# Attention: the row maxima of two heads taken by one instruction over two neighbouring PSUM banks

## The chip, the cores and the metric

The kernel is one program on one core of a Trainium2 chip. Its five engines (TensorE, the matmul engine, PE in the profile; VectorE, DVE; ScalarE, ACT; GpSimd, POOL; SyncE, SP) each run their own list of instructions in order, and wait for each other through semaphores. The metric is the device time of one execution in microseconds (us); of the kernel before there are three runs, and one further execution with the profiler on, which all rows below come from.

## The reference, cut to what matters

The whole is two gated blocks on 32 sequences of 100 tokens of width 256: cross-attention, a mixture of experts routed by a recurrence (GRU), an alignment step, and a second mixture of experts. The change is in the first, the cross-attention, whose core is:

```python
q = (query @ Wq.T + bq).reshape(B, -1, HEADS, HEAD_DIM)     # 32 x 100 x 16 heads x 16
k = (key @ Wk.T + bk).reshape(B, -1, HEADS, HEAD_DIM)       # 32 x 361 x 16 x 16
v = (value @ Wv.T + bv).reshape(B, -1, HEADS, HEAD_DIM)
scores = jnp.einsum('bqhd,bkhd->bhqk', q, k) * scale
attn = jax.nn.softmax(scores, axis=-1)
out = jnp.einsum('bhqk,bkhd->bqhd', attn, v).reshape(B, -1, DIM)
return out @ Wo.T + bo
```

The softmax takes away each row's maximum over the 361 keys before the exponential: a maximum for each of 100 queries, 16 heads and 32 batches. The kernel's scores carry a negative scale, so that the maximum is taken as a minimum, and the exponential runs with scale -1.

## The kernel before, in words

Function `attention` (from L242) works batch by batch, 32 in all, and within a batch head by head, 16 slots h = 0 to 15. The order of each engine's instructions is written out by hand: on each engine a function `turn_of(b, u, first, last)` runs through the 16 slots, and a table of constants (L265 to L270) says in which slot what happens. The work is a software pipeline: while the heads of batch b are turned and multiplied, the projections of batch b+1 and the last steps of batch b-1 lie in between.

The life of one head:

- `scores` (L565): TensorE makes the scores of a group of four heads at a time. Each takes a strip of 32 rows of the array, so the four run side by side; each writes its own PSUM bank, `score[0]` to `score[3]`, 100 x 361 in float32. This happens in slots h = 2, 6, 10, 14, for the group that begins two slots later (in slot 6 heads 8 to 11; in slot 14 heads 0 to 3 of the next batch). It waits until the exponentials of the whole group before are done (`p_ready`), because these read the same four banks.
- `maximum` (L453): VectorE reduces one bank, 100 x 361, to 100 x 1 in `neg_max`. It waits for the score of its head (`s_psum`) and for the use of its place in `neg_max` eight heads earlier.
- `exponential` (L377): ScalarE writes the exponentials of the bank to `probs`, once the head's maximum is there (`max_ready`).
- `turn_probs` (L576): TensorE transposes `probs` in three parts of 121 keys (slot h for head h), when the exponential is done.
- The turned head is copied to `probsT`, an even head by VectorE (L505) and an odd one by ScalarE (`odd_out`, L387).
- `outputs` (L584): four heads times the values, 24 small matmuls, once a group.

Beside these a batch has: `project_keys`, `project_queries`, `project_values` for the next batch; `turn_back`, `divide` (reciprocal and product on VectorE, L462 and L464), `turn_attn`, `project_output` and the statistics for the batch before.

On VectorE a slot begins with the copy of an even head; then come the maxima that `MAXIMA[h % 4]` names, counted from the first head of the current group (4 and above is the next group); then the slot's other work. `MAXIMA = ((3,), (), (4,), (5, 6))` means: the first head of a group gets its maximum in slot 2 of the group before, the second and third in slot 3, and the fourth only in the next slot 0, after the copy of the even head there. ScalarE has the same kind of table: in slot 3 (after the copy of the odd head) the exponential of the next group's first head, in slot 0 the second and third, in slot 1 the fourth.

Of the kernel before, what the change touches and what calls it, by code (L numbers as in the profile page):

```python
# [7 lines left out]
F32 = mybir.dt.float32  # L8
# [3 lines left out]
ALU = mybir.AluOpType  # L12
ACT = mybir.ActivationFunctionType
AX = mybir.AxisListType

P = 128
B, S, DIM = 32, 100, 256
KV, KC = 361, 121
# [3 lines left out]
HEADS, HD = 16, 16  # L22
# [201 lines left out]
def at_least(engine, semaphore, value):  # L224

    if not isinstance(value, int) or value > 0:
        engine.wait_ge(semaphore, value)
# [14 lines left out]
def attention(nc, rows, mean, rstd, ctxT, weights, weights_in, x_rows, ident,  # L242
# [10 lines left out]
    with ExitStack() as ctx:  # L253
        def sb(name, shape, dt=F32):
            return ctx.enter_context(nc.sbuf_tensor("att_" + name, shape, dt))

        def ps(name):
            return ctx.enter_context(nc.psum_tensor("att_" + name, [P, 512], F32))

        def sem(name):  # L260
            return ctx.enter_context(nc.semaphore("att_" + name))

        BANKS, KEPT = 4, 8
# [2 lines left out]
        KEYS, VALUES = (1, 9), (11, 13, 15)  # L266
        FIRST_OUTPUTS, OUTPUTS = 4, {8: 1, 12: 2}
        SCORES = 2
        MAXIMA = ((3,), (), (4,), (5, 6))
        EXPONENTIALS = ((1, 2), (3,), (), (4,))  # L270
        wq, wk, wv, wo, bq_bk, mask_sb, bv_all, bo_gated, gate = weights
        c_in = [sb(f"c_in{u}", [P, KT, KVP]) for u in range(2)]
# [7 lines left out]
        neg_max = sb("neg_max", [S, KEPT])  # L280
# [4 lines left out]
        attn = sb("attn", [S, HEADS, HD])  # L285
        attnT = sb("attnT", [P, KT, S])

        score = [ps(f"score{n}") for n in range(BANKS)]
        turned = [ps(f"turned{n}") for n in range(2)]
        outs = ps("outs")  # L290
        misc = ps("misc")
# [9 lines left out]
        s_psum, max_ready, p_ready = sem("s_psum"), sem("max_ready"), sem("p_ready")  # L301
# [13 lines left out]
        def head_at(b, u, h, last):  # L315

            if h < HEADS:
                return b, u, h
            return None if last else (b + 1, 1 - u, h - HEADS)
# [116 lines left out]
        def _(dve):  # L436
            def normalized(b):
                at_least(dve, xnT_psum, b)
                normalize(nc, xn[:], rows_of(b), mean, rstd, b).then_inc(xn_ready, 1)

            def queries_out(b):
                dve.wait_ge(q_psum, b + 1)
                at_least(dve, q_ready, b)
                nc.vector.tensor_tensor(q_all[:], misc[:, 0:KT * S].rearrange("p (g s) -> p g s", g=KT),  # L444
                                        bq_bk[:, 0, :].unsqueeze(2).to_broadcast([P, KT, S]), ALU.add).then_inc(q_copied, 1)

            def values_out(b, u, m):
                dve.wait_ge(v_psum, 3 * b + m + 1)
                at_least(dve, o_psum, HG * b - HG)
                nc.vector.tensor_tensor(v[u][:, m, :, 0:HD], misc[0:KC, 0:DIM].rearrange("p (h d) -> p h d", h=HEADS),  # L450
                                        bv_all[0:KC, :].rearrange("p (h d) -> p h d", h=HEADS), ALU.add).then_inc(v_ready, 1)

            def maximum(b, u, h):  # L453
                dve.wait_ge(s_psum, HEADS * b + h + 1)
                at_least(dve, p_ready, HEADS * b + h + 1 - KEPT)
                nc.vector.tensor_reduce(neg_max[:, h % KEPT:h % KEPT + 1], score[h % BANKS][0:S, 0:KV], AX.X, ALU.min).then_inc(max_ready, 1)  # L456

            def divide(b):

                dve.wait_ge(back_psum, b + 1)  # L460
                heads = misc[0:S, :].rearrange("p (h j) -> p h j", h=HEADS)
                nc.vector.reciprocal(inverse[:], heads[:, :, HD]).then_inc(inverse_ready, 1)  # L462
                dve.wait_ge(inverse_ready, b + 1)
                nc.vector.tensor_tensor(attn[:], heads[:, :, 0:HD], inverse[:].unsqueeze(2).to_broadcast([S, HEADS, HD]),  # L464
                                        ALU.mult).then_inc(attn_ready, 1)

            def add_output(b, u):
                dve.wait_ge(bias_added, b + 1)
                dve.wait_ge(y_psum, b + 1)
                nc.vector.scalar_tensor_tensor(x1[u][:], misc[0:S, DIM:2 * DIM], gate[0:S, 0:1], rows_of(b),  # L470
                                               ALU.mult, ALU.add).then_inc(x1_ready, 1)

            def keep_output(b, u):
                dve.wait_ge(x1_ready, b + 1)
                at_least(dve, aggregated, b)
                nc.vector.tensor_scalar(rows_of(b), x1[u][:], 1.0, None, ALU.mult).then_inc(x1_kept, 1)
                nc.vector.bn_stats(stats[:], x1[u][:]).then_inc(stats_done, 1)

            def statistics_taken(b):
                dve.wait_ge(stats_done, b + 1)  # L480
                at_least(dve, stats_kept, b)

            def aggregate(b):
                nc.vector.bn_aggr(mean_var_now[:], stats[:]).then_inc(aggregated, 1)

            def keep_statistics(b):
                dve.wait_ge(aggregated, b + 1)
                nc.vector.tensor_scalar(mean_var[:, bass.ds(b, 1), :].rearrange("p a n -> p (a n)"), mean_var_now[:], 1.0, None, ALU.mult).then_inc(stats_kept, 1)
# [5 lines left out]
            queries_out(0)  # L494
            for m in range(3):
                values_out(0, 0, m)
            for h in range(3):
                maximum(0, 0, h)

            def turn_of(b, u, first, last):  # L500
                for h in range(HEADS):
                    if h % 2 == 0:
                        dve.wait_ge(t_psum, HEADS * b + h + 1)
                        at_least(dve, o_psum, HG * b + h // 4 - 1)
                        nc.vector.tensor_copy(probsT[h // 4 % 2][:, h % 4, :], turned[0][0:KC, 0:3 * S]).then_inc(even_ready, 1)  # L505
                    if h == TURN - 4 and not last:
                        normalized(b + 1)
                    for r in MAXIMA[h % 4]:
                        head = head_at(b, u, h - h % 4 + r, last)
                        if head:  # L510
                            maximum(*head)
                    if h == BACK and not first:
                        divide(b - 1)
                    if h == OUTPUT + 2 and not first:
                        statistics_taken(b - 1)
                    if h in VALUES and not last:
                        values_out(b + 1, 1 - u, VALUES.index(h))
                    if h == OUTPUT and not first:
                        add_output(b - 1, 1 - u)
                    if h == QUERIES and not last:  # L520
                        queries_out(b + 1)
                    if h == OUTPUT + 1 and not first:
                        keep_output(b - 1, 1 - u)
                    if h == OUTPUT + 2 and not first:
                        aggregate(b - 1)
                    if h == OUTPUT + 3 and not first:
                        keep_statistics(b - 1)

            pipelined(dve, B, turn_of)
            divide(B - 1)  # L530
            add_output(B - 1, 1)
# [2104 lines left out]
```

## Time and profile before

| | |
|---|---|
| time, median of 3 runs | 3348.98 us (3347.38 to 3350.77) |
| time of the profiled execution | 3356.15 us |
| its span, first to last instruction | 3354.5 us |
| mean granted TensorE clock | 0.945 |
| TensorE matmul busy, whole span | 2969.9 us (89%) |
| VectorE busy | 1424.3 us (42%) |
| ScalarE busy | 958.9 us (29%) |
| row maxima (L456) | 512 instructions, 250.1 us |

The attention stage lies in the first 750 us of the span. A start in the rows is in microseconds from the span's start; the number after it is the duration, of all merged instructions together where there are several (the x at the end is their count). Square brackets give how long the engine had been idle before and who released it. Busy TensorE time includes the overlap of one matmul with the next, so a short delay on TensorE can show as no idle time at all.

### The profile page before, as it was taken

The page shows a single profiled execution, that of the slowest core. Times are in us where ns is not written, and L with a number is a line of the kernel's source. Part 1 is how long each engine was busy: PE and PEld are TensorE (multiplying, and loading weights), DVE is VectorE, ACT ScalarE, POOL GpSimd, SP SyncE. Part 2 cuts the span into 40 slices and gives each one's busy share as a digit, 9 for nine tenths or more (in the row PEclk, how much of TensorE's full clock was granted, in tenths as well). Part 3 has the DMA queues.
Part 4 walks back from the last instruction along what each step waited for, and adds up shares of the span by engine and source line. Part 5 has one row for each costly group of instructions (what it writes and reads, how often), then busy time and mean ns, then how long its engine had stood idle before and what let it go on. Part 6 is the DMA issues. An engine that isn't in the chain of part 4 may idle for free. (4 is left out here: it accounts for less than half of the span.)

```text
span 3354.5 us, 72380 instructions
## 1 busy us (share of the span) xinstructions
PE 2969.9 (89%) x27712; PEld 1662.2 (50%) x27713; DVE 1424.3 (42%) x3167; ACT 958.9 (29%) x2643; POOL 815.3 (24%) x771
## 2 busy tenths in 40 slices
PE   5999999988999999999999999999999976008698
PEld 3666666653444444444444444458666644007454
DVE  4666666652222233333323333345222246985311
ACT  2555555543111111111111111122122236472111
POOL 1111001100222222232222222233444422004243
PEclk9999999987999999999999999999999988558699
DMA  6000000003000000000000000041222253005143
GB/s 225 24 21 20 21 23 23 23 11 128 23 16 23 17 23 17 23 17 17 22 17 23 17 23 17 23 176 53 43 45 45 45 148 119 0 0 198 46 115 72
DMA packets 81216, 163.02 MB, mean 49 GB/s; under 512 B 12056, under 2 KB 54936, under 8 KB 76408
## 3 DMA queue, kind: packets, MB, share of 16 engines
q1 hardware_dynamic: 55848, 102.34, 9.7%
q0 software_dynamic: 21504, 40.67, 5.5%
q10 hardware_dynamic: 3664, 17.04, 1.4%
q8 instruction: 162, 2.65, 0.3%
q14 instruction: 38, 0.31, 0.0%
HBM read 119.63 MB, written 40.37 MB: 48 GB/s over the span
## 5 line engine op out<-in xcount | busy, mean ns | idle before, releaser
L926 PE MATMUL gru_ps_rz<-whh,scratch 128*32 128x512 f32 x6400 | 707.4, 594 | 0.0
L734 POOL TENSOR_TENSOR scratch<-scratch 128x1024 f32<-128x1024 f32 (+3 forms) x246 | 369.6, 1527 | 818.5 <-DVE stat L748 657.6
L926 PEld LDWEIGHTS gru_ps_rz<-whh,scratch 128*32 128x32 f32 x6400 | 197.7, 110 | 452.1 <-issue 452.1
L931 PE MATMUL gru_ps_n<-whh,scratch 128*32 128x256 f32 x6400 | 363.6, 379 | 0.0
L855 DVE TENSOR_TENSOR scratch<-scratch,state 128x256 f32<-128x256 f32 x100 | 50.8, 508 | 661.1 <-ACT scratch L884 661.1
L931 PEld LDWEIGHTS gru_ps_n<-whh,scratch 128*32 128x32 f32 x6400 | 207.9, 110 | 180.1 <-issue 59.8
L380 ACT ACTIVATE att_probs<-att_score,att_neg_max 100x361 f32<-100x361 f32 x512 | 260.6, 568 | 122.2 <-DVE att_neg_max L456 122.1
L581 PEld LDWEIGHTS att_turned<-ident,att_probs 100*121 100x121 f32 x1536 | 210.3, 185 | 140.3 <-issue 105.9
L581 PE MATMUL att_turned<-ident,att_probs 100*121 100x100 f32 x1536 | 267.3, 287 | 11.8 <-ACT att_probs L380 5.0
L456 DVE TENSOR_REDUCE att_neg_max<-att_score 100x1 f32<-100x361 f32 x512 | 250.1, 525 | 56.0 <-PE att_score L573 56.0
L884 ACT ACTIVATE scratch<-gru_ps_rz 128x512 f32<-128x512 f32 x100 | 59.7, 597 | 720.3 <-PE gru_ps_rz L926 720.3
L903 PE MATMUL gru_ps_rz<-wih,scratch 128*32 128x512 f32 x1600 | 191.5, 596 | 2.2 <-POOL scratch L823 2.2
L2219 PE MATMUL e_ps_g<-align_reach,ident 32*121 32x101 f32 x64 | 10.9, 326 | 196.8 <-DVE align_reach L2031 195.3
L748 DVE TENSOR_REDUCE stat<-scratch 128x2048 f32 (+3 forms) x96 | 181.1, 1886 | 0.0
L505 DVE COPY att_probsT<-att_turned 121x300 f32<-121x300 f32 x256 | 119.0, 465 | 134.3 <-PE att_turned L581 134.1
L887 ACT ACTIVATE scratch<-scratch 128x256 f32<-128x256 f32 x100 | 41.7, 417 | 349.0 <-DVE scratch L859 349.0
L390 ACT COPY att_probsT<-att_turned 121x300 f32<-121x300 f32 x256 | 103.5, 404 | 131.9 <-PE att_turned L581 131.9
L857 DVE TENSOR_TENSOR scratch<-scratch,gru_ps_n 128x256 f32<-128x256 f32 x100 | 42.1, 421 | 231.7 <-PE gru_ps_n L931 231.7
L573 PE MATMUL att_score<-att_kT,att_qT 32*100 32x361 f32 x1024 | 112.3, 508 | 16.1 <-ACT att_probs L380 15.4
L356 POOL TENSOR_TENSOR att_qT<-att_q_all,att_head_mask 128x400 f32<-128x400 f32 x32 | 27.3, 853 | 379.8 <-DVE att_q_all L444 379.7
L1470 DVE COPY mix_room<-mix_ps_m 128x512 f32<-128x512 f32 x57 | 39.4, 691 | 187.7 <-PE mix_ps_m L1559 187.7
L1147 POOL DMA_INDIRECT x<-mix_room,mix_rows_listed x57 | 90.4, 1586 | 92.1 <-ACT mix_room L1205 87.6
(377 smaller groups left out, 4385.2 us busy)
## 6 DMA issues: line engine op xcount, KB each, us to landing
table<-in_w SPq DMA_DIRECT2D x16, 1024.0 KB, 7.0
states<-state SPq DMA_DIRECT2D x100, 128.0 KB
scratch<-states SPq DMA_DIRECT2D x25, 512.0 KB, 3.6
whh<-in_whhT POOLq DMA_DIRECT2D x8, 1536.0 KB, 17.3
att_c_in<-in_ctxT SPq DMA_DIRECT2D x32, 363.0 KB, 3.0
dist_ctx<-in_ctxT SPq DMA_DIRECT2D x32, 363.0 KB, 5.5
align_ctx<-in_ctx_rows SPq DMA_DIRECT2D x32, 363.0 KB
whh<-in_guT ACTq DMA_DIRECT2D x8, 1024.0 KB, 12.1
```

What stands on the lines that cost most here:

```text
L380: nc.scalar.activation(probs[h % KEPT][:, 0:KV], score[h % BANKS][0:S, 0:KV], ACT.Exp, bias=neg_max[:, h % KEPT:h % KEPT + 1], scale=-1.0) ...
L390: nc.scalar.copy(probsT[h // 4 % 2][:, h % 4, :], turned[1][0:KC, 0:3 * S]).then_inc(odd_ready, 1)
L456: nc.vector.tensor_reduce(neg_max[:, h % KEPT:h % KEPT + 1], score[h % BANKS][0:S, 0:KV], AX.X, ALU.min).then_inc(max_ready, 1)
L505: nc.vector.tensor_copy(probsT[h // 4 % 2][:, h % 4, :], turned[0][0:KC, 0:3 * S]).then_inc(even_ready, 1)
L573: nc.tensor.matmul(score[r][0:S, 0:KV], qT[u][strip, half, g, :], kT[u][strip, g, 0:KV], start=True, stop=True).then_inc(s_psum, 1)
L581: done = nc.tensor.transpose(turned[h % 2][0:KC, m * S:(m + 1) * S], probs[h % KEPT][:, m * KC:(m + 1) * KC], ident[0:S, 0:S])
L734: done = nc.gpsimd.tensor_tensor(last.prod[:, row:row + rows, :], a, b, ALU.mult)
L748: nc.vector.tensor_reduce(stat[:, bass.ds(it, 1), at:at + rows].rearrange("p a n -> p (a n)"), last.prod[:, 0:rows, :], AX.X, ALU.add).the ...
L903: nc.tensor.matmul(ps_rz[quarter(q), :], xt[u][:, k, j, :], rz_columns(wih, k, q), start=(k == 0), stop=False)
L926: last = nc.tensor.matmul(ps_rz[quarter(q), :], stateT[c % 2][:, quarter(c // 2)], rz_columns(whh, c, q), start=False, stop=(c == GC - 1))
L931: last = nc.tensor.matmul(ps_n[quarter(q), 0:GQ], stateT[c % 2][:, quarter(c // 2)], n_columns(whh, c, q), start=(c == 0), stop=(c == GC - 1))
L1147: nc.gpsimd.indirect_dma_start(x2, bass.IndirectOffsetOnAxis(ap=rows_listed[:, n:n + 1], axis=0), y[u], None, compute_op=ALU.add).then_inc ...
```

## The change

It makes the four score banks one PSUM tensor of 128 x 4 x 512, in which bank n is a slice (same place, same size), and replaces `maximum`, one head an instruction, by `maxima`, two heads an instruction: 100 x 2 x 361 in, 100 x 2 out. It waits for the score of the second of the two heads, and adds 2 to `max_ready` when it ends. The table becomes `((), (), (4,), (6,))`: the pair of heads 4 and 5 in slot 2 (of each four), the pair 6 and 7 in slot 3, nothing in slot 0. So the fourth head of a group is no longer done in the next slot 0, but in slot 3 together with the third, and the second is done with the first in slot 2. Ahead of the loop two pairs replace three single maxima. The instructions of TensorE, ScalarE, GpSimd and SyncE are as before.

```diff
-        MAXIMA = ((3,), (), (4,), (5, 6))
+        MAXIMA = ((), (), (4,), (6,))
...
-        score = [ps(f"score{n}") for n in range(BANKS)]
+        score_banks = ctx.enter_context(nc.psum_tensor("att_score", [P, BANKS, 512], F32))
+        score = [score_banks[:, n, :] for n in range(BANKS)]
...
-            def maximum(b, u, h):
-                dve.wait_ge(s_psum, HEADS * b + h + 1)
-                at_least(dve, p_ready, HEADS * b + h + 1 - KEPT)
-                nc.vector.tensor_reduce(neg_max[:, h % KEPT:h % KEPT + 1], score[h % BANKS][0:S, 0:KV], AX.X, ALU.min).then_inc(max_ready, 1)
+            def maxima(b, u, h):
+                dve.wait_ge(s_psum, HEADS * b + h + 2)
+                at_least(dve, p_ready, HEADS * b + h + 2 - KEPT)
+                nc.vector.tensor_reduce(neg_max[:, h % KEPT:h % KEPT + 2], score_banks[0:S, h % BANKS:h % BANKS + 2, 0:KV], AX.X,
+                                        ALU.min).then_inc(max_ready, 2)
...
-            for h in range(3):
-                maximum(0, 0, h)
+            for h in (0, 2):
+                maxima(0, 0, h)
...
-                            maximum(*head)
+                            maxima(*head)
```

## Rows read from the trace of the kernel before

**Rows 1.** Busy time by engine in 100 us: PE, PEld, DVE, ACT, POOL, clock.

```profile
250.00:350.00 100.00, 95.64 (x1003) 68.59 (x996) 66.52 (x165) 58.57 (x136) 9.48 (x13) 1.00 0.08 23
```

**Rows 2.** Waits between 100 and 600 us: total, times, longest.

```profile
ACT att_probs L380 <- DVE att_neg_max L456: 81.2, 69, 1.7
PE att_score L573 <- ACT att_probs L380: 11.0, 23, 0.5
```

**Rows 3.** Timeline from slot 6 to slot 10 of one batch, three engines.

```profile
299.86 0.87 PE L573 MATMUL att_score<-att_kT,att_qT 32*100 32x361 f32 x8 [0.48 <-ACT att_probs L380]
...
300.75 1.41 DVE L456 TENSOR_REDUCE att_neg_max<-att_score 100x1 f32<-100x361 f32 x3 [0.85 <-PE att_score L573]
...
301.05 1.06 PE L555 MATMUL att_misc<-att_xnT,att_wq 128*128 128x100 f32 x8
301.25 0.41 ACT L390 COPY att_probsT<-att_turned 121x300 f32<-121x300 f32 x1 [0.69 <-PE att_turned L581]
301.56 1.47 ACT L380 ACTIVATE att_probs<-att_score,att_neg_max 100x361 f32<-100x361 f32 x3
...
302.25 0.55 PE L581 MATMUL att_turned<-ident,att_probs 100*121 100x100 f32 x3
...
303.79 1.41 PE L548 MATMUL att_misc<-att_c_in,att_wk 128*128 128x363 f32 x4
...
305.04 0.46 PE L581 MATMUL att_turned<-ident,att_probs 100*121 100x100 f32 x3
```

**Rows 4.** Timeline, slot 14 to slot 0 of the next batch.

```profile
311.07 0.87 PE L573 MATMUL att_score<-att_kT,att_qT 32*100 32x361 f32 x8
...
312.04 0.53 DVE L456 TENSOR_REDUCE att_neg_max<-att_score 100x1 f32<-100x361 f32 x1 [0.17 <-PE att_score L573]
...
312.26 1.05 PE L561 MATMUL att_misc<-att_wv,att_c_in 128*121 128x256 f32 x4
312.46 0.41 ACT L390 COPY att_probsT<-att_turned 121x300 f32<-121x300 f32 x1 [1.30 <-PE att_turned L581]
...
312.77 1.47 ACT L380 ACTIVATE att_probs<-att_score,att_neg_max 100x361 f32<-100x361 f32 x3
...
313.39 0.56 PE L581 MATMUL att_turned<-ident,att_probs 100*121 100x100 f32 x3
```

**Rows 5.** Timeline, slot 2 to slot 6 of that batch.

```profile
316.57 0.87 PE L573 MATMUL att_score<-att_kT,att_qT 32*100 32x361 f32 x8
...
317.54 1.42 DVE L456 TENSOR_REDUCE att_neg_max<-att_score 100x1 f32<-100x361 f32 x3 [0.39 <-PE att_score L573]
...
318.26 1.47 ACT L380 ACTIVATE att_probs<-att_score,att_neg_max 100x361 f32<-100x361 f32 x3
...
319.15 0.42 DVE L464 TENSOR_TENSOR att_attn<-att_misc,att_inverse 100x256 f32<-100x256 f32 x1
319.17 0.88 PE L581 MATMUL att_turned<-ident,att_probs 100*121 100x100 f32 x6
...
319.76 0.47 DVE L505 COPY att_probsT<-att_turned 121x300 f32<-121x300 f32 x1 [0.19 <-PE att_turned L581]
...
320.15 0.52 DVE L456 TENSOR_REDUCE att_neg_max<-att_score 100x1 f32<-100x361 f32 x1
320.29 0.56 PE L581 MATMUL att_turned<-ident,att_probs 100*121 100x100 f32 x3
...
320.71 0.56 ACT L380 ACTIVATE att_probs<-att_score,att_neg_max 100x361 f32<-100x361 f32 x1 [0.97 <-DVE att_neg_max L456]
...
321.33 0.87 PE L573 MATMUL att_score<-att_kT,att_qT 32*100 32x361 f32 x8 [0.48 <-ACT att_probs L380]
```

**Rows 6.** VectorE's reductions by shape: count, total us, mean ns.

```profile
L456 DVE TENSOR_REDUCE att_neg_max<-att_score 100x1 f32<-100x361 f32 x512 | 250.1, 525 | 56.0 <-PE att_score L573 56.0
...
L748 DVE TENSOR_REDUCE stat<-scratch 128x16 f32<-128x2048 f32 x1 | 2.3, 2276 | 0.0
...
L748 DVE TENSOR_REDUCE stat<-scratch 128x10 f32<-128x1280 f32 x1 | 1.5, 1479 | 0.0
```

**Rows 7.** Timeline, slot 10 to slot 12, VectorE and ScalarE.

```profile
306.31 1.42 DVE L456 TENSOR_REDUCE att_neg_max<-att_score 100x1 f32<-100x361 f32 x3 [0.31 <-PE att_score L573]
```

## The prediction, made before the changed kernel was run

> **What bounds the kernel now.** I read the busy time by stretch first. In the attention stage TensorE is busy 95.6 us of 100, VectorE 66.5, ScalarE 58.6 [rows 1]: TensorE sets the pace, and neither of the engines that the change touches is full. Then the waits: ScalarE stands long for the maxima, 81.2 us of 500, and TensorE for an exponential, 11.0 us in 23 times [rows 2]. Only the second kind can move the end, so I went to the timeline of one batch to see where TensorE really waits.
>
> Matmuls overlap, so the bare gap misleads. Where TensorE is never held up, a transposed head begins 0.16 us before the group ahead has ended: keys 303.79 + 1.41 = 305.20, next head 305.04 [rows 3]. Against that measure three places of a batch are held up by the chain score, maximum, exponential:
>
> - Slot 8: the queries end at 302.11, the head would begin at 301.95, it begins at 302.25 [rows 3]. Head 8's exponential (301.56, and 0.57 long, since three take 1.47 at a step of 0.45) ends at 302.13. Held up 0.30 us.
> - Slot 0: values end at 313.31, the head would begin at 313.15, it begins at 313.39 [rows 4], just after head 0's exponential (312.77 + 0.57 = 313.34). Held up 0.24 us.
> - Slot 6: the scores of heads 8 to 11 wait for head 7's exponential, 320.71 + 0.56 = 321.27, and start at 321.33, where the head before them ended at 320.85 [rows 5]. With the overlap before scores in the free case (about 0.07: their tile shape differs, and 320.29 + 0.56 - 0.07 = 320.78 is where they would begin) that is 0.55 us. Since 299.86, the same point a batch before, 21.47 us have passed.
>
> **What the change removes and adds.** 512 reductions of 361 elements become 256 of 722. The price of a pair isn't in the trace. The nearest rows: one bank takes 0.525 us; with several outputs, 2048 elements take 2.276 and 1280 take 1.479 us, so an element costs 0.797 / 768 = 1.04 ns [rows 6]. A pair is 0.525 + 361 x 1.04 ns = 0.90 us. Its bounds: 0.75 (722 elements and no fixed part at all) and 1.05 (the fixed part paid anew at the second bank). I take 0.90, since ten and sixteen outputs in one reduction show no extra price against that slope. Reductions in a row start 0.445 us apart (three take 1.42) [rows 5], so two give way to one that holds the engine for 0.90 - 0.08 = 0.82 us: 0.07 us of VectorE saved a pair. By itself this is worth nothing, as VectorE is a third idle; what counts is when each maximum is there.
>
> The first head of each group gets its maximum later: it was done after 0.53 us and is now done with the second, after 0.90 us, 0.37 us later. The second head's comes 0.07 us earlier. The fourth's comes much earlier: it no longer waits for the next slot 0.
>
> *Slot 8.* The pair starts at 300.75 and ends at 301.65. The exponential of head 8 starts later than the maximum by a lag. Seen for a group's first head are 0.28 (301.28 to 301.56 [rows 3]) and 0.20 (312.57 to 312.77 [rows 4]); both are bounds from above, because the exponential also starts 0.305 us after the copy ahead of it in both. The bound from below is 0.04: 320.15 + 0.52 = 320.67 to 320.71 [rows 5]. The new start is between 301.69 and 301.93, against 301.56; I take a lag of 0.25, nearer to the cases of a first head: 301.90, 0.34 late. TensorE was already waiting here, so all of it is lost: +0.34 us (0.13 to 0.37).
>
> *Slot 0.* Pair 312.04 to 312.94, lag 0.20 at most, exponential at 313.14 in place of 312.77, and again TensorE already waits: +0.37 us (0.21 to 0.37). The values' addition, queued behind the second pair on VectorE, ends some 0.35 us later, and the keys that need it come more than a microsecond after; nothing.
>
> *Slots 2 to 6.* The pair for heads 4 and 5 ends at 317.54 + 0.90 = 318.44, head 4's exponential starts at 318.64 in place of 318.26 and ends at 319.21, so the two turned heads (319.17 before) start at about 319.26, the second at 319.71 in place of 319.56, held by the exponential of head 5. Behind the second pair on VectorE are now reciprocal and product, 0.31 us later (the product ends at 319.88, which TensorE needs only at about 320.0), and the copy of head 4, 319.86 in place of 319.76. The turn of head 6 thus slips from 320.29 to 320.39 or 320.40. But head 7's maximum is long there: its exponential follows head 6's at about 319.98 and ends at 320.55. The scores then start right behind head 6, at 320.88 in place of 321.33: -0.45 us (from -0.55, if nothing slips, to -0.30, if the delays of head 5 and of the copy add up).
>
> *Slot 12.* The pair starts at 306.31 [rows 7] and ends at 307.21, which puts head 12's exponential about 0.1 us later; its turn comes more than half a microsecond after that exponential's end, so nothing is lost.
>
> *Whole batch.* +0.34 + 0.37 - 0.45 = +0.26 us, some 31.5 times over the stage: +8.2 us. One thing more: the first maximum starts 0.88 us after the scores in slots 6 (299.86 to 300.75) and 0.97 in slots 14 and 2 (311.07 to 312.04, 316.57 to 317.54) [rows 3 to 5]. The pair waits for other counts of the same semaphores, so slot 6 may come to behave like the others: up to 0.09 x 32 = 2.9 us more; at even odds +1.4. Sum: +9.6 us, on the profiled execution 3356.15 to 3365.8 us. That execution is 7.2 us above the median of the runs, in which I see nothing that belongs to this stage, so I add the same difference to the median: 3348.98 + 9.6 = 3358.6 us.
>
> **A rule against this sum.** VectorE is two thirds busy here [rows 1]. The Trainium skill, *Perfetto Trace Analysis*, in its section "Optimizing Scalar/DVE Operations", says that larger, grouped operations can improve throughput if the engine is saturated, with an overhead per instruction of about 125 ns for DVE on PSUM. By it 256 instructions fewer would be an estimated 32 us of VectorE; the condition isn't met, so by the same sentence nothing reaches the end. No row here shows 125 ns.
>
> **The rivals.**
>
> 1. *Faster: the early fourth maximum wins.* The stall of slot 6 is the longest, and it is the one that goes. If the lags at the first heads were short (0.04 in both places) and a pair cost 0.80, slot 8 would lose 0.03 and slot 0 0.11 (the copies ahead then bind), slots 2 to 6 win 0.55: -0.4 us a batch, -13 us, 3336 us. For it speaks that these lags are known only as bounds; against it the slope of 1.04 ns, which has no room for 0.80. It decides from a first-head delay under 0.22 us. Chance 0.10.
> 2. *No change that can be measured: the two sides cancel.* A pair of 0.86, or lags in between, give +0.1 us a batch, +3 us, 3352 us. Chance 0.27.
> 3. *Much slower: the second bank costs a fixed part again*, 1.05 us a pair. Each of the three places moves by 0.15 more: +0.26 + 0.45 = 0.7 us a batch, +22 us, 3371 us. Nothing in the rows has two banks in one instruction. Chance 0.06.
>
> **How the numbers follow.** The forecast (+7 to +16 us, slower) has 0.57, rival 3 0.06, rival 2 0.27, rival 1 0.10. The likeliest is 3358.6 us, its own range 3355 to 3365. Leaving out most of rivals 1 and 3 the range is 3349 to 3368. What this measurement can tell from no change is about 0.2%, 6.7 us: my central value is only just past it. Slower by more than 0.2%: 0.63; within: 0.28; faster: 0.09.
>
> **What would show it.** In the changed trace: reductions of 100x722 x256 at 0.90 us mean; a batch of 21.7 us between the scores of slot 6; these scores without the 0.48 idle; the head in slot 8 some 2.75 us after the scores of slot 6 (2.39 before), and in slot 0 2.69 after those of slot 14 (2.32 before); VectorE's reduction time from 250 to 230 us. I am wrong if the pair's length is off 0.90 by more than 0.05, if ScalarE starts a first exponential within 0.1 us of the pair's end, or if the scores of slot 6 find another wait.

## The result

The changed kernel takes 3358.57 us in the median of 18 runs (3352.83 to 3364.85), the one before 3350.49 (18 runs, 3345.26 to 3356.31). The ratio is 1.0027, 95% interval 1.002 to 1.0033: a little slower, by 8 us, against 9.6 forecast. The profiled execution has a span of 3356.4 us, only 1.9 more than the one before. But that one was long outside this stage, as the prediction supposed: from the first score matmul to the last group of scores 690.2 us passed before (44.18 to 734.37) and 698.5 now (42.66 to 741.13), 8.3 more, while all the rest of the span fell from 2664.3 to 2657.9, and lies between 2655 and 2662 in every other trace.

Busy time in the same 100 us as [rows 1], now of the changed kernel; the columns are the length, then PE, PEld, DVE, ACT, POOL, clock, DMA share, GB/s:

```profile
250.00:350.00 100.00, 94.31 (x1005) 68.19 (x1006) 62.77 (x127) 59.94 (x137) 9.48 (x13) 1.00 0.08 23
```

VectorE has less to do (62.8 in place of 66.5) and TensorE still gets less done (94.3 in place of 95.6). The reductions, against the first row of [rows 6], and then the waits, against [rows 2]:

```profile
L457 DVE TENSOR_REDUCE att_neg_max<-att_score 100x2 f32<-100x722 f32 x256 | 223.0, 905 | 56.2 <-PE att_score L575 55.8 <-issue 0.4
```

```profile
PE att_turned L583 <- ACT att_probs L381: 22.5, 46, 0.6
...
ACT att_probs L381 <- DVE att_neg_max L457: 17.4, 57, 0.3
```

A pair costs 0.905 us (0.90 forecast), 27 us of busy VectorE are saved over the stage, and ScalarE's long waits for maxima have gone from 81.2 to 17.4 us. TensorE's wait for the scores of slot 6, 11.0 us in 23 times, has gone from the list; in its place it waits 22.5 us in 46 times, twice a batch, for the first exponential of a group, where the kernel before had this row:

```profile
PE att_turned L581 <- ACT att_probs L380: 1.9, 12, 0.2
```

By the prediction's measure TensorE was held there before too, and the overlap hid most of it. That is the exchange the prediction describes. The timeline of slots 6 to 8, which answers to [rows 3]:

```profile
301.38 0.87 PE L575 MATMUL att_score<-att_kT,att_qT 32*100 32x361 f32 x8
...
302.46 1.72 DVE L457 TENSOR_REDUCE att_neg_max<-att_score 100x2 f32<-100x722 f32 x2 [0.51 <-PE att_score L575]
302.57 1.06 PE L557 MATMUL att_misc<-att_xnT,att_wq 128*128 128x100 f32 x8
302.77 0.41 ACT L391 COPY att_probsT<-att_turned 121x300 f32<-121x300 f32 x1 [0.97 <-PE att_turned L583]
303.49 1.92 ACT L381 ACTIVATE att_probs<-att_score,att_neg_max 100x361 f32<-100x361 f32 x4 [0.30 <-DVE att_neg_max L457]
...
304.18 0.56 PE L583 MATMUL att_turned<-ident,att_probs 100*121 100x100 f32 x3 [0.55 <-ACT att_probs L381]
```

The queries end at 303.63, and head 8 begins only at 304.18, 2.80 us behind its scores where it was 2.39. The four exponentials now run in one row. This is a batch of odd number. In the next one the pair of slot 6 starts sooner, 0.98 us behind the scores and not 1.08, it ends at 325.14, and the exponential follows 0.03 us later, not 0.11:

```profile
323.25 0.87 PE L575 MATMUL att_score<-att_kT,att_qT 32*100 32x361 f32 x8
...
324.23 1.73 DVE L457 TENSOR_REDUCE att_neg_max<-att_score 100x2 f32<-100x722 f32 x2 [0.40 <-PE att_score L575]
...
325.17 1.47 ACT L381 ACTIVATE att_probs<-att_score,att_neg_max 100x361 f32<-100x361 f32 x3
```

Head 8 is turned 2.80 us behind the scores in odd batches and 2.62 in even ones. Slots 14 to 0, against [rows 4]:

```profile
312.99 0.87 PE L575 MATMUL att_score<-att_kT,att_qT 32*100 32x361 f32 x8
...
314.07 0.91 DVE L457 TENSOR_REDUCE att_neg_max<-att_score 100x2 f32<-100x722 f32 x1 [0.40 <-PE att_score L575]
...
315.10 1.47 ACT L381 ACTIVATE att_probs<-att_score,att_neg_max 100x361 f32<-100x361 f32 x3 [0.30 <-DVE att_neg_max L457]
315.71 0.45 PE L583 MATMUL att_turned<-ident,att_probs 100*121 100x100 f32 x2 [0.48 <-ACT att_probs L381]
```

And slots 2 to 6, against [rows 5]:

```profile
318.89 0.87 PE L575 MATMUL att_score<-att_kT,att_qT 32*100 32x361 f32 x8
...
319.97 1.73 DVE L457 TENSOR_REDUCE att_neg_max<-att_score 100x2 f32<-100x722 f32 x2 [0.50 <-PE att_score L575]
...
321.61 1.01 PE L583 MATMUL att_turned<-ident,att_probs 100*121 100x100 f32 x6
...
321.90 0.42 DVE L466 TENSOR_TENSOR att_attn<-att_misc,att_inverse 100x256 f32<-100x256 f32 x1
...
322.80 0.51 PE L583 MATMUL att_turned<-ident,att_probs 100*121 100x100 f32 x3
...
323.25 0.56 PE L575 MATMUL att_score<-att_kT,att_qT 32*100 32x361 f32 x4
```

The scores of slot 6 come 4.35 us behind those of slot 2, without a wait, where they came 4.76 behind.

For all comparisons below I took the same intervals out of each trace, as means over the middle batches. *Start* is from the scores to the first reduction, *lag* from the end of that reduction to the first exponential, *turn* from the scores to the turned head that needs it; *2 to 6* is from scores to scores. Times in us, ratios with their intervals in the text. Where odd and even batches differ, the table has their mean: for the changed kernel and late_fourth, start 6 is 1.08 and 0.98, lag 6 is 0.11 and 0.03, turn 8 is 2.80 and 2.62.

| kernel | batch | start 6 / 14 | lag 6 / 14 | turn 8 / 0 | 2 to 6 | ratio |
|---|---|---|---|---|---|---|
| before | 21.50 | 0.88 / 0.97 | 0.28 / 0.19 | 2.39 / 2.36 | 4.76 | 1 |
| changed | 21.81 | 1.03 / 1.08 | 0.07 / 0.11 | 2.70 / 2.76 | 4.35 | 1.0027 |
| layout_only | 21.50 | 0.88 / 0.97 | 0.28 / 0.19 | 2.39 / 2.36 | 4.76 | 0.9998 |
| late_fourth | 22.34 | 1.03 / 1.08 | 0.07 / 0.11 | 2.70 / 2.76 | 4.88 | 1.0071 |
| early_single | 21.12 | 0.88 / 0.97 | 0.28 / 0.19 | 2.40 / 2.36 | 4.37 | 0.9951 |
| pair_swapped | 21.60 | 0.99 / 0.99 | 0.07 / 0.11 | 2.67 / 2.67 | 4.26 | 1.0010 |
| pair_both | 21.45 | 0.93 / 0.93 | 0.11 / 0.12 | 2.64 / 2.61 | 4.21 | 0.9996 |
| early_swapped | 21.03 | 0.88 / 0.88 | 0.28 / 0.28 | 2.40 / 2.36 | 4.28 | 0.9955 |
| early_exp_only | 20.82 | 0.88 / 0.97 | 0.07 / 0.11 | 2.18 / 2.27 | 4.37 | 0.9925 |
| early_exp_first | 20.53 | 0.88 / 0.88 | 0.04 / 0.04 | 2.14 / 2.11 | 4.28 | 0.9912 |
| pair_exp_first | 21.29 | 0.93 / 0.93 | 0.04 / 0.04 | 2.56 / 2.52 | 4.21 | 0.9980 |
| tail_pair | 20.46 | 0.88 / 0.88 | 0.04 / 0.04 | 2.14 / 2.11 | 4.22 | 0.9891 |

The changed batch is 0.31 us longer, times 31 that is 9.7 us; the stage grew by 8.3, as the first and last batches run otherwise. Its parts: slot 8 +0.31, slot 0 +0.40, slots 2 to 6 -0.40.

### The profile page after: what moved, and what is told of

It reads as the page before. It is cut to its first block and busy times, and to the rows that moved or that the text cites. A ratio compares the mean times of both kernels' runs of the same rounds, so it can differ in the third digit from the quotient of the medians.

```text
span 3356.4 us, 71966 instructions
## 1 busy us (share of the span) xinstructions
PE 2964.9 (88%) x27712; PEld 1660.9 (49%) x27713; DVE 1402.3 (42%) x2911; ACT 967.0 (29%) x2643; POOL 815.4 (24%) x771
## 5 line engine op out<-in xcount | busy, mean ns | idle before, releaser
L381 ACT ACTIVATE att_probs<-att_score,att_neg_max 100x361 f32<-100x361 f32 x512 | 249.9, 563 | 39.6 <-DVE att_neg_max L457 33.0
L457 DVE TENSOR_REDUCE att_neg_max<-att_score 100x2 f32<-100x722 f32 x256 | 223.0, 905 | 56.2 <-PE att_score L575 55.8
## 6 DMA issues: line engine op xcount, KB each, us to landing
whh<-in_whhT POOLq DMA_DIRECT2D x8, 1536.0 KB, 17.4
```

Source lines behind the costliest of these rows:

```text
L381: nc.scalar.activation(probs[h % KEPT][:, 0:KV], score[h % BANKS][0:S, 0:KV], ACT.Exp, bias=neg_max[:, h % KEPT:h % KEPT + 1], scale=-1.0) ...
L457: nc.vector.tensor_reduce(neg_max[:, h % KEPT:h % KEPT + 2], score_banks[0:S, h % BANKS:h % BANKS + 2, 0:KV], AX.X, ALU.min).then_inc(max_ ...
```

## The experiments

**The joined tensor alone (layout_only).**

```diff
-        score = [ps(f"score{n}") for n in range(BANKS)]
+        score_banks = ctx.enter_context(nc.psum_tensor("att_score", [P, BANKS, 512], F32))
+        score = [score_banks[:, n, :] for n in range(BANKS)]
```

> The kernel before with the four score banks as one PSUM tensor, and still one head an instruction in the old order. Arrival theory (the time follows when each group's first and fourth maximum arrives): ratio to before 1.000, within 0.001, and a batch of 21.50 us as before. Rival (the joined tensor itself costs, by waits or by place): some or all of the 1.0027 of the changed kernel shows here.

Measured 0.9998 (0.9988 to 1.0007), every interval as before. The joined tensor costs nothing.

**The gain without the pair (early_single).**

```diff
-        MAXIMA = ((3,), (), (4,), (5, 6))
+        MAXIMA = ((), (), (4,), (5, 6, 7))
...
-            for h in range(3):
+            for h in range(4):
                 maximum(0, 0, h)
```

> The kernel before with one head an instruction, but the fourth maximum moved into the slot of the third: the gain of the change without its pair. Arrival theory: the scores of slot 6 start about 0.38 us earlier against those of slot 2 (4.76 us before, 4.38 to 4.40 now), the slots 8 and 0 stay at 2.39 and 2.32 us behind their scores; 31 x 0.38 = 12 us less, ratio 0.9965. Rival (fewer and larger reductions are what VectorE needs; the order is indifferent): 512 reductions as before, ratio 1.000.

Measured 0.9951 (0.9938 to 0.9965), 3334.17 us in the median. The batch is 0.386 us shorter, all of it between slots 2 and 6; 12 us of the 17 measured follow from that, the rest lies within the interval. Its VectorE:

```profile
250.00:350.00 100.00, 97.98 (x1027) 70.60 (x1025) 67.70 (x173) 58.60 (x137) 10.78 (x15) 1.00 0.07 20
```

VectorE is busier than in the changed kernel (67.7 against 62.8) and TensorE gets more done. The rival that counts VectorE's load falls.

**The loss without the gain (late_fourth, against the changed kernel).**

```diff
-        MAXIMA = ((), (), (4,), (6,))
+        MAXIMA = ((3,), (), (4,), (6,))
...
-            for h in (0, 2):
-                maxima(0, 0, h)
+            maxima(0, 0, 0)
+            maximum(0, 0, 2)
...
-                            maxima(*head)
+                            (maxima if r == 4 else maximum)(*head)
```

(with `maximum` kept from the kernel before beside `maxima`)

> The changed kernel with only the first two heads of a group as a pair; the third alone in its slot, the fourth alone and late, as before: the loss of the change without its gain. Arrival theory: slots 8 and 0 late by 0.40 us each as in the changed kernel, and the scores of slot 6 a further 0.1 us late through head 4: 31 x 0.9 = 28 us more than before, ratio 1.008 to 1.009. Rival (VectorE's load decides): 384 reductions, less VectorE work than before, ratio between 1.000 and 1.0027.

Measured 1.0071 (1.0057 to 1.0085); the batch is 0.84 us longer, of which slot 8 +0.31, slot 0 +0.40 and slots 2 to 6 +0.12. Slot 8 is again less than the 0.40 expected: it is +0.40 in odd batches and +0.22 in even ones. The wait of [rows 5] is back in its place:

```profile
328.42 0.56 ACT L381 ACTIVATE att_probs<-att_score,att_neg_max 100x361 f32<-100x361 f32 x1 [0.69 <-DVE att_neg_max L463]
329.03 0.87 PE L580 MATMUL att_score<-att_kT,att_qT 32*100 32x361 f32 x8 [0.48 <-ACT att_probs L381]
```

**Why the pair starts late: the order of its waits (pair_swapped, then pair_both).** In the changed kernel a pair starts 1.08 us after its scores, and 0.98 in slot 10 and in slot 6 of even batches. The instruction records of slot 2 show what lies between: the wait for the scores sits on a register operation (it computes the value of the next wait), then comes a wait instruction of its own for `p_ready`, then the reduction: 319.821, 319.909 and 319.974 us. Where it is 0.98, the register operation runs ahead of the waits, and both sit on one wait instruction.

```diff
             def maxima(b, u, h):
-                dve.wait_ge(s_psum, HEADS * b + h + 2)
                 at_least(dve, p_ready, HEADS * b + h + 2 - KEPT)
+                dve.wait_ge(s_psum, HEADS * b + h + 2)
```

> The changed kernel with its two waits in the other order: first the wait for the place in neg_max (long fulfilled), then the wait for the scores. In the changed kernel the first pair starts 1.08 us after its scores, where single maxima started 0.88 or 0.97 us after; I put this down to register and semaphore instructions between the wait for the scores and the reduction. If so, the pair starts 0.89 us after the scores in all slots, slots 8 and 0 gain 0.19 us each and slot 6 up to 0.1: 31 x 0.38 to 0.48 = 12 to 15 us less than the changed kernel, ratio to before 0.998 to 0.999. Rival (a read over two banks starts later, whatever stands before it): no change, ratio 1.0027.

Measured 1.001 (1.0001 to 1.0019). The start is 0.99 in every slot: from 1.08 that is half of what I expected, and where it had been 0.98 nothing was gained. The direction was right, the size not. The timeline of slots 2 and 6:

```profile
315.87 0.87 PE L575 MATMUL att_score<-att_kT,att_qT 32*100 32x361 f32 x8
...
316.86 1.73 DVE L457 TENSOR_REDUCE att_neg_max<-att_score 100x2 f32<-100x722 f32 x2 [0.42 <-PE att_score L575]
...
320.13 0.87 PE L575 MATMUL att_score<-att_kT,att_qT 32*100 32x361 f32 x8
```

A separate wait instruction was still there, 0.065 us ahead of the reduction. So, the increment (pair_both, against pair_swapped):

```diff
-                                        ALU.min).then_inc(max_ready, 2)
+                                        ALU.min).then_inc(max_ready, 1)
...
-                act.wait_ge(max_ready, HEADS * b + h + 1)
+                act.wait_ge(max_ready, HEADS // 2 * b + h // 2 + 1)
```

> pair_swapped once more, and each pair adds 1 to max_ready in place of 2 (ScalarE waits for 8 a batch). pair_swapped started its pairs at 0.99 us, not 0.89; what is left I put down to the add of 2, which leaves the reduction no room for a wait of its own. If so, the pair starts 0.89 us after its scores, slots 8 and 0 gain 0.10 us each and slot 6 a few hundredths: 31 x 0.2 to 0.25 = 6 to 8 us less than pair_swapped, ratio to before 0.9985 to 0.999. Rival (two banks in one read, or the wait for the second head, cost these 0.10 us): no change against pair_swapped, ratio 1.001.

Measured 0.9996 (0.9987 to 1.0004), by the two ratios some 5 us less than pair_swapped; the intervals overlap a little, but the traces agree, with a batch 0.15 us shorter. The start is 0.93, the wait instruction is gone from the records, and the reduction waits for the scores itself:

```profile
314.98 0.87 PE L575 MATMUL att_score<-att_kT,att_qT 32*100 32x361 f32 x8
315.91 1.73 DVE L457 TENSOR_REDUCE att_neg_max<-att_score 100x2 f32<-100x722 f32 x2 [0.35 <-PE att_score L575]
```

Of the 0.10 us expected 0.07 is gone. 0.04 remains against a single maximum, and it is the wait for the second head: the trace has the times at which the count of `s_psum` rises, 0.860 us after the scores' start for the first head and 0.902 for the second, and single maximum and pair alike start 0.023 us after the count that they need. Nothing is left for the second bank. (In slot 6 of even batches the exponential's lag rose from 0.04 to 0.11, as ScalarE's wait for the maximum now sits on a register operation there too, which takes back a part.) With both edits the changed kernel is level with the one before.

**What holds the first exponential (early_swapped, early_exp_only, early_exp_first).** The lags, 0.28 and 0.19 before and 0.03 or 0.11 with a pair, can't be a fixed latency.

> early_single with the two waits of the maxima in the other order. First theory (the first exponential of a group is held by ScalarE's copy ahead of it, 0.305 us from start to start, not by its maximum): the maximum of slots 14 and 2 starts 0.09 us earlier, no exponential moves, ratio to before 0.995 as early_single. Rival (the lags of 0.19 and 0.28 us are a latency from the maximum to the exponential, and stay): slots 0 and 4 gain 0.09 us, 31 x 0.09 to 0.15 = 3 to 5 us less, ratio 0.994.

(early_single with the same swap in `maximum`.) Measured 0.9955 (0.9942 to 0.9968). No exponential of slots 8 and 0 moved: the start fell by 0.09 in slot 14 and the lag rose by 0.09. The trace does show a batch 0.09 us shorter, through slots 2 to 6: in early_single TensorE turns `attn` 0.06 us after VectorE's product ends, so it now waits for the product (in the changed kernel 0.14 us lie between, in the kernel before 0.31), and with the swap the product and the scores of slot 6 both come 0.09 us sooner. The first theory had not named that, and the measured times can't tell it. Then the copy (early_exp_only, against early_single):

```diff
-                    if h % 4 == 3:
+                    if h % 8 == 3:
                         odd_out(b, h)
                     for r in EXPONENTIALS[h % 4]:
...
-                    if h % 4 == 1:
+                    if h % 4 == 1 or h % 8 == 7:
                         odd_out(b, h)
```

> early_single with ScalarE's first exponential of a group before, not behind, the copy of the odd head in slots 7 and 15 (elsewhere as it was). If the lag were the copy alone, slots 8 and 0 would gain up to 0.25 us each, ratio 0.991. If behind the copy the register work between the wait for the maximum and the exponential is just as long (0.19 to 0.26 us), the order changes at most 0.03 us a slot, ratio 0.995. I expect the second.

Measured 0.9925 (0.9913 to 0.9937). I expected 0.03 us a slot at most, and was wrong: slot 8 comes 0.21 us earlier and slot 0 0.09. The copy was most of the lag; what lies behind the maximum is 0.11 us where the wait sits on a register operation and 0.03 where the exponential waits itself, not 0.19 to 0.26. Then with the late wait last in both functions (early_exp_first):

```diff
             def exponential(b, u, h):
-                act.wait_ge(max_ready, HEADS * b + h + 1)
                 at_least(act, t_psum, HEADS * b + h + 1 - KEPT)
+                act.wait_ge(max_ready, HEADS * b + h + 1)
...
             def maximum(b, u, h):
-                dve.wait_ge(s_psum, HEADS * b + h + 1)
                 at_least(dve, p_ready, HEADS * b + h + 1 - KEPT)
+                dve.wait_ge(s_psum, HEADS * b + h + 1)
```

> early_exp_only, with the waits of the maxima and of the exponentials in the order that puts the late one last (places in neg_max and probs first, then scores and maxima). Theory: the lag falls from 0.19 to 0.28 us to 0.04, the turned heads of slots 8 and 0 come 0.25 us earlier each, as far as TensorE lets them (2.10 us behind their scores in place of 2.39 and 2.36): 31 x 0.5 = 15 us less than early_single, ratio to before 0.990 to 0.991. Rival (TensorE is not held by these exponentials): ratio 0.995.

Measured 0.9912 (0.99 to 0.9925), 3319.82 us. The lag is 0.04, slots 8 and 0 stand at 2.14 and 2.11, and TensorE is all but full:

```profile
250.00:350.00 100.00, 99.25 (x1043) 72.08 (x1043) 68.18 (x174) 60.59 (x141) 10.45 (x15) 1.00 0.08 24
```

**The price of the pair, all else equal (pair_exp_first).** Both pairs put into that kernel (pair_both, with the exponential's two edits):

> early_exp_first with both pairs (each adds 1), so all else equal: the price of the pair at the head of the group alone. Arrival theory: the first exponential waits for 0.91 in place of 0.53 us of reduction, the turned heads of slots 8 and 0 come at 2.57 and 2.54 us behind their scores in place of 2.14 and 2.11, slot 6 changes by less than 0.1: a batch of 21.2 to 21.4 us, 31 x 0.8 = 25 us more than early_exp_first, ratio to before 0.998. Rival (with the waits in order and the exponential first the pair is hidden): a batch within 0.2 us of early_exp_first, ratio 0.992.

Measured 0.998 (0.9971 to 0.9988); a batch of 21.29 us against 20.53, slots 8 and 0 later by 0.42 and 0.41. Of each, 0.38 is the longer first reduction and 0.04 the wait for the second head's score:

```profile
318.25 1.73 DVE L457 TENSOR_REDUCE att_neg_max<-att_score 100x2 f32<-100x722 f32 x2 [0.35 <-PE att_score L575]
319.19 0.56 ACT L381 ACTIVATE att_probs<-att_score,att_neg_max 100x361 f32<-100x361 f32 x1 [1.54 <-DVE att_neg_max L457]
319.88 0.56 PE L583 MATMUL att_turned<-ident,att_probs 100*121 100x100 f32 x3 [0.31 <-ACT att_probs L381]
```

**The pair where nobody waits for its first half (tail_pair).** early_exp_first, the joined tensor, and the swapped-wait `maxima` of pair_swapped beside `maximum`, for the third and fourth head alone (ahead of the loop too, which is left out here):

```diff
-        MAXIMA = ((), (), (4,), (5, 6, 7))
+        MAXIMA = ((), (), (4,), (5, 6))
...
-                            maximum(*head)
+                            (maxima if r == 6 else maximum)(*head)
```

> early_exp_first with a pair where nobody waits for its first half: heads 4 and 5 of each four alone, heads 6 and 7 as a pair. Arrival theory: no first maximum is delayed, VectorE reaches reciprocal and product 0.07 us earlier at most: a batch of 20.45 to 20.53 us against 20.525, ratio to before 0.990 to 0.9915. Rival (a read over two banks disturbs others, or any pair costs): a batch longer than 20.6 us.

Measured 0.9891 (0.9874 to 0.9909), 3315.10 us in the median, the fastest of all; the batch is 20.46 us, and the 0.07 us saved between slots 2 and 6 is just the term by which a pair is shorter than two singles: VectorE's product, which TensorE waits for, comes that much sooner. By the traces the pair pays there. The measured times don't show it, since the intervals of this kernel and of early_exp_first overlap.

```profile
322.85 0.97 DVE L457 TENSOR_REDUCE att_neg_max<-att_score 100x1 f32<-100x361 f32 x2 [0.31 <-PE att_score L581]
323.67 2.03 ACT L381 ACTIVATE att_probs<-att_score,att_neg_max 100x361 f32<-100x361 f32 x4
323.75 0.90 DVE L462 TENSOR_REDUCE att_neg_max<-att_score 100x2 f32<-100x722 f32 x1
```

## Why the prediction was right, step by step

- *What binds.* Right. TensorE sets the pace, and the three places named were where the time moved: late_fourth has the two losses without the gain, early_single the gain without the losses.
- *A pair takes 0.90 us.* Right, 0.905. The slope from reductions over other shapes held over two banks, and rival 3 falls. The "250 to 230 us" set busy time merged (250) against a sum (256 x 0.90); merged, it is now 223.0.
- *Slot 8, +0.34.* +0.31 on average. The sum was right, two terms were not: the lag was 0.07 on average (taken 0.25), and the pair started 0.15 us later than a single maximum (at most 0.09 allowed for). That they cancel is luck.
- *Slot 0, +0.37.* +0.40, with the same pair of errors: start +0.11, lag 0.11 in place of 0.20. My "0.20 at most" for the lag held; nothing had been allowed for the start there.
- *Slots 2 to 6, -0.45.* -0.40. The late start pushed head 4 and all behind it; with the swap (pair_swapped) the interval is 4.26, so the forecast 4.31 was undercut once the start was mended.
- *Its own sign of error.* The prediction called itself wrong if ScalarE starts a first exponential within 0.1 us of the pair's end. It does: 0.03 us in slot 10 and in slot 6 of even batches. So the lag was mis-sized by the prediction's own test, and the sum came out because the late start made up for it: with the start at 0.93 (pair_both) no slowdown is left, where +7 us was the least forecast. The other signs (the pair's length, no new wait for the scores of slot 6) stayed away.
- *Slot 12, nothing.* Right: 5.64 us from the scores of slot 10 to those of 14 in all kernels.
- *The start might move, +1.4 us over the stage.* Right as a worry, mis-sized: swapping the waits and counting by one give back 0.36 us a batch, 11 us. What I had read as a property of slots (0.88 here, 0.97 there) is the number of instructions between the wait for the scores and the reduction.
- *3358.6 us.* Measured 3358.57; that this is so near is luck. The median before, over 18 runs, is 1.5 us above the one of 3 runs that I added to, and the difference is 8.1 us where I had 9.6. A batch grew by 0.31 us (0.26, and 0.04 for the start, forecast), but 31.5 times that is more than the stage's 8.3. The profiled execution, forecast at 3365.8, took 3358.39.
- *The rule on grouping.* The Trainium skill, *Perfetto Trace Analysis*, "Optimizing Scalar/DVE Operations", has grouping pay if the engine is saturated. The changed kernel agrees: VectorE was not saturated, and 27 us less of its busy time did not shorten it. But saturation is not the whole of it: in tail_pair VectorE is no more saturated (69 of 100 us), and by the traces the merge still gains 0.07 us a batch, since TensorE waits for what VectorE does next. Rival 1, which gave the gain of slot 6 the upper hand, needed short lags and a cheaper pair; the lags were nearly that short, but the pair took 0.905, and the late start took the place of the lags.

## What to carry to other kernels

An instruction over two items hands over both at the end of the second, so merge only where nobody waits for the first; here the same merge cost 0.77 us a batch with both pairs of each group and, by the traces, paid 0.07 at the tail alone. Separate an edit that merges from the reordering that comes with it: here the reordering was worth 12 us and the merging took more than that back. Where an engine waits for several things, let it wait last for the one that comes last, and look at how far its start is from the release, not only at the releaser's name.

## What was not expected of the hardware

- Between a fulfilled wait and the reduction behind it lay up to two more sequencer instructions, 0.09 us for a register operation and 0.065 us for a separate wait. Swapping two waits, with no other edit, took 0.09 us off the pair's start in slots 14 and 2 and in slot 6 of odd batches; in slot 6 of even ones and in slot 10, where the register operation already ran ahead, it took nothing.
- A reduction that adds 2 to a semaphore had its wait in an instruction of its own ahead of it, in all 256 of the changed kernel; with an increment of 1 it waits itself (all 256 of pair_both), and starts 0.07 us earlier.
- The counts of four score matmuls that run side by side rise 0.042 us apart, though the matmuls start 0.007 us apart in the records; a pair waits for the second of them.
- A ScalarE copy of 121x300 ahead of an exponential holds it back for 0.305 us from start to start; putting the exponential first (early_exp_only) was worth 0.21 us in slot 8.
